# Small-head attention: per-head products of 32 rows in place of masked key copies, slots written out

## The reference

```python
scores = jnp.einsum('bqhd,bkhd->bhqk', Q, K) / scale     # 16 heads, d = 8
attn = jax.nn.softmax(scores, axis=-1)
out = jnp.einsum('bhqk,bkhd->bqhd', attn, V).reshape(B, T_q, D)
```

## Time and profile before

| | us |
|---|---|
| median of 3 runs | 1088.5 |
| lowest, highest | 1086.8, 1091.34 |
| span of the profiled execution | 1088.4 |
| TensorE matmuls busy | 889.5 |
| VectorE busy | 787.4 |
| ScalarE busy | 470.4 |
| GpSimd busy | 172.3 |

### The profile page before, as it was taken

One profiled execution on the slowest core, in us unless ns is written; L12 is line 12 of the kernel. 1 busy time (PEld: TensorE's weight loads), 2 busy tenths in 40 slices (PEclk: granted clock), 3 DMA queues, 4 the chain that ended last, 5 costly groups with the idle time before them and its releaser, 6 DMA issues. The chain is left out here.

```text
span 1088.4 us, 15120 instructions
## 1 busy us (share of the span) xinstructions
PE 889.5 (82%) x5078; PEld 654.4 (60%) x5078; DVE 787.4 (72%) x1420; ACT 470.4 (43%) x693; POOL 172.3 (16%) x139
## 2 busy tenths in 40 slices
PE   2688747767998998899966888469989975999997
PEld 2555535436676676777744555346766754777774
DVE  4688654766868767678876887768677665778875
ACT  1254422113454443289941545134544422555553
POOL 1000010003313222122230000133132211011112
PEclk9699966997999999699975999679999985999998
DMA  7000000030000000000110050000000000000000
GB/s 321 1 1 1 1 0 1 0 155 1 1 0 0 0 1 2 0 1 0 36 43 0 1 244 4 0 1 1 1 0 0 1 1 0 1 0 0 0 1 20
DMA packets 1916, 22.78 MB, mean 21 GB/s; under 512 B 208, under 2 KB 208, under 8 KB 1104
## 3 DMA queue, kind: packets, MB, share of 16 engines
q1 hardware_dynamic: 1872, 22.22, 5.0%
HBM read 21.69 MB, written 0.52 MB: 20 GB/s over the span
## 5 line engine op out<-in xcount | busy, mean ns | idle before, releaser
L180 PE MATMUL banks<-work_split 128*128 128x256 f32 (+1 forms) x420 | 153.7, 366 | 13.1 <-DVE work_split L1186 6.8
L180 PE MATMUL banks<-normed_t_high,work_split 128*128 128x512 f32 x260 | 113.7, 437 | 46.2 <-DVE normed_tokens L924 9.9
L181 PE MATMUL banks<-work_split 128*128 128x256 f32 (+1 forms) x420 | 140.3, 334 | 0.0
L182 PE MATMUL banks<-work_split 128*128 128x256 f32 (+1 forms) x420 | 140.2, 334 | 0.0
L855 POOL TENSOR_TENSOR work<-work 128x512 f32<-128x512 f32 x64 | 86.4, 1350 | 260.3 <-PE banks L700 167.0
L180 PEld LDWEIGHTS banks<-work_split 128*128 128x128 f32 x420 | 82.0, 195 | 65.4 <-issue 30.0
L182 PE MATMUL banks<-normed_t_high,work_split 128*128 128x512 f32 x260 | 107.7, 414 | 0.0
L181 PE MATMUL banks<-normed_t_low,work_split 128*128 128x512 f32 x260 | 107.3, 413 | 0.0
L524 DVE TENSOR_REDUCE work<-banks 128x2 f32<-128x512 f32 x128 | 84.9, 687 | 27.3 <-PE banks L359 26.9
L180 PEld LDWEIGHTS banks<-normed_t_high,work_split 128*128 128x128 f32 x260 | 51.4, 198 | 67.3 <-issue 27.4
L182 PEld LDWEIGHTS banks<-work_split 128*128 128x128 f32 x420 | 82.1, 196 | 7.9
(11 more groups left out here) (228 smaller groups left out, 1816.9 us busy)
## 6 DMA issues: line engine op xcount, KB each, us to landing
raw_b<-in_wf SPq DMA_DIRECT2D x1, 6528.0 KB, 19.6
raw_a<-in_wf SPq DMA_DIRECT2D x1, 4096.0 KB, 12.0
raw_a<-in_wf SPq DMA_DIRECT2D x1, 2048.0 KB, 13.0
raw_b<-in_wb SPq DMA_DIRECT2D x1, 2048.0 KB, 17.5
raw_a<-in_wb SPq DMA_DIRECT2D x1, 2048.0 KB, 7.9
small_operands<-in_small SPq DMA_DIRECT2D x1, 1600.0 KB, 7.1
residual<-in_x SPq DMA_DIRECT2D x1, 512.0 KB, 3.7
sublayer_out_t<-in_ctx_t SPq DMA_DIRECT2D x1, 512.0 KB, 7.9
```

The costliest lines, as they stand in the source:

```text
L180: nc.tensor.matmul(o, w[0], m[0], start=start, stop=False)
L181: nc.tensor.matmul(o, w[0], m[1], start=False, stop=False)
L182: return nc.tensor.matmul(o, w[1], m[0], start=False, stop=stop)
```

## The change

- The four masked copies are gone. The keys stay in one stacked buffer `a_ky`, now with four halves (the keys of steps x to x + 3), and the ones of rows 24 and 25 are added by ACT as a bias in `high`.
- A product for head j reads the 32 partitions of head j alone, of weights and of moving data, both in `maxima` and in `scores`.
- `maxima(x, n)` is one head (n % 4) with two query tiles of one sequence instead of one tile with two heads.
- `scores(x, u)` is one pair of heads with both key blocks of one sequence; head j always writes bank j. Scores 2 and 3 wait for the exponentials of 0 and 1. There are four probability buffers instead of two (two lie in `raw_a`, columns 6144 to 8191), and `values(x, b)` has eight products for a sequence instead of four: two groups per slot instead of four.
- The first four projections use banks 4, 5, 2 and 3, and do not wait for stacks.
- All eight slots of a call are written out, on PE, ACT and DVE.

```diff
-        A = signals("a", NG, w=2, q=4, hi=4, y=4, km=8, v=2, mx=16, red=16, m2=2, mt=2, yf=2, s=8, p=8, pv=8,
+        A = signals("a", NG, w=2, q=4, hi=4, y=4, v=2, mx=16, red=16, m2=2, mt=2, yf=2, s=8, p=8, pv=4,
...
-        a_y, a_yf, a_ky = wr[:, 0:1024], wr[:, 1024:2048], wr[:, 2048:3072]
-        a_km = [wr[:, 3072 + 1024 * j:4096 + 1024 * j] for j in range(GH)]
+        a_y, a_yf, a_ky = wr[:, 0:1024], wr[:, 1024:2048], wr[:, 2048:4096]
...
+        a_p += [raw_a[:, 6144 + 1024 * k:7168 + 1024 * k] for k in range(2)]
...
-        def small_passes(eng, slot):
-
-
-            with eng.Fori(0, NG - 2) as i:
-                slot(i, 0, True, True, True)
-                slot(i, 1, True, True, True)
-            slot(NG - 2, 0, True, True, True)
-            slot(NG - 2, 1, False, True, True)
-            slot(NG - 1, 0, False, False, True)
-            slot(NG - 1, 1, False, False, False)
+
+
+        STEPS = 2 * NG
+
+        def a_rows(j):
+            return slice(BLK * j, BLK * (j + 1))
+
+        def a_bank(x, k):
+
+            return (4, 5, 2, 3)[2 * x + k] if x < 2 else 5
...
+                if k and x >= 2:
+                    at("y", 2 * x + 1)
...
+                mm3(bank(a_bank(x, k)), (a_wh[:, k * P:(k + 1) * P], a_wl[:, k * P:(k + 1) * P]), src)\
+                    .then_inc(A["q"].sem, 1)
...
+            def maxima(x, n):
+                pair, j = n // GH, n % GH
                 if n == 0:
-                    at(i, "km", 4 * x + 4)
+                    at("y", 2 * x + 2)
                 if n >= 2:
-                    at(i, "red", 8 * x + n - 1)
-                for j in range(j0, j0 + 2):
-                    last = nc.tensor.matmul(ps[:, 6 + n % 2, (j % 2) * S:(j % 2 + 1) * S],
-                                            a_y[:, t * P:(t + 1) * P], a_km[j][:, (t // 2) * S:(t // 2 + 1) * S],
+                    at("red", 8 * x + n - 1)
+                for e in range(2):
+                    t = 4 * (x % 2) + 2 * pair + e
+                    last = nc.tensor.matmul(ps[:, 6 + n % 2, e * S:(e + 1) * S], a_y[a_rows(j), t * P:(t + 1) * P],
+                                            half(a_ky, x % 4)[a_rows(j), pair * S:(pair + 1) * S],
                                             start=True, stop=True)
                 last.then_inc(A["mx"].sem, 1)
...
             def scores(x, u):
+                b = u // 2
+                if u >= 2:
+                    at("p", 4 * x + u - 1)
+                for kb in range(2):
+                    for j in range(2 * (u % 2), 2 * (u % 2) + 2):
+                        last = nc.tensor.matmul(ps[:, j, kb * S:(kb + 1) * S],
+                                                half(a_ky, x % 4)[a_rows(j), b * S + kb * P:b * S + (kb + 1) * P],
+                                                half(a_yf, x % 2)[a_rows(j), b * S:(b + 1) * S],
+                                                start=True, stop=True)
...
+            def values(x, b):
+                if b == 0:
+                    at("v", x + 1)
+                at("p", 4 * x + 2 * b + 2)
+                for kb in range(2):
+                    for j in range(GH):
+                        last = nc.tensor.matmul(ps[a_rows(j), 4, b * S:(b + 1) * S],
+                                                a_vg[:, 4 * (x % 2) + 2 * b + kb, j, :],
+                                                a_p[2 * b + j // 2][:, (2 * (j % 2) + kb) * S:(2 * (j % 2) + kb + 1) * S],
+                                                start=kb == 0, stop=kb == 1)
...
+            def slot(x):
                 def more(*tiles):
+                    for n in tiles if x + 1 < STEPS else ():
+                        maxima(x + 1, n)
+
+                at("yf", x + 1)
                 scores(x, 0)
                 more(0, 1)
                 scores(x, 1)
                 more(2)
+                scores(x, 2)
                 more(3)
+                if x + 2 < STEPS:
+                    project(x + 2, 1)
                 more(4)
+                values(x, 0)
                 scores(x, 3)
+                more(5, 6, 7)
+                values(x, 1)
+                if x + 2 < STEPS:
+                    at("y", 2 * (x + 2) + 2)
+                sums_back(x)
+                if x + 1 < STEPS:
+                    maxima_back(x + 1)
+                if x + 3 < STEPS:
+                    at("att", x + 1)
+                    project(x + 3, 0)
...
+                at("q", 2 * x + k + 1)
+                if x >= 1:
+                    at("y", 2 * (x - 1) + k + 1)
+                src = bank(a_bank(x, k))
+                if k:
+                    ins = nc.scalar.activation(half(a_hi, k), src, ACT.Identity, bias=col("one_rows"))
+                else:
+                    ins = nc.scalar.activation(half(a_hi, k), src, ACT.Copy)
+                ins.then_inc(A["hi"].sem, 1)
...
+                    if u == 3 and x + 2 < STEPS:
+                        high(x + 2, 1)
+                    at("s", 4 * x + u + 1)
+                    if x:
+                        at("pv", 2 * (x - 1) + u // 2 + 1)
+                    nc.scalar.activation(a_p[u], bank(2 * (u % 2), 2), ACT.Exp,
                                          scale=float(1.0 / np.sqrt(np.float32(DH8)))).then_inc(A["p"].sem, 1)
+                at("pv", 2 * x + 2)
...
+                dst = half(a_ky, x % 4) if k else half(a_y, x % 2)
...
-            def masked_keys(i, x, heads=range(GH)):
-                at(i, "y", 2 * x + 2)
-                for j in heads:
-                    nc.vector.tensor_scalar(half(a_km[j], x % 2), half(a_ky, x % 2).bitcast(F32), col("one_rows"),
-                                            col("head", j, 1), ALU.add, ALU.mult).then_inc(A["km"].sem, 1)
...
+                t, j = 4 * (x % 2) + 2 * (n // GH), n % GH
...
+                if x % 2 == 1 and x // 2 + 2 < NG:
+                    small_weights(dve, c, x // 2 + 2, raw, r0)
...
+                if x + 1 < STEPS:
+                    minus(x + 1)
+                normalise(x)
+                if x + 1 < STEPS:
+                    queries(x + 1)
...
+    ones = ((r % BLK == 24) | (r % BLK == 25)).astype(f)[:, None]
+    put("lo_k", ones - ((r % BLK) // DH8 == 1).astype(f)[:, None])
+    put("one_rows", ones)
```

More of the change, by code:

```diff
@@ L405, in slot @@
                 more(2)
+                scores(x, 2)
                 more(3)
[L407 to L410, removed]
+                if x + 2 < STEPS:
+                    project(x + 2, 1)
                 more(4)
-                values(i, x, 1)
-                more(5)
+                values(x, 0)
                 scores(x, 3)
[L415 to L426, removed]
+                more(5, 6, 7)
[8 more added lines that the diff above has]
+                    project(x + 3, 0)
             for x in range(2):
                 pe.wait_ge(s_xs, 2 * splits(m) + x + 1)
[L430 to L433, removed]
+                project(x, 0)
+                project(x, 1)
             for n in range(8):
[L435 to L439, removed]
+                maxima(0, n)
+            maxima_back(0)
+            project(2, 0)
+            for x in range(STEPS):
+                slot(x)
         def small_act(act, c):
@@ L447, in small_act, with at @@
             vsrc = vsrc.rearrange("p (t d) -> p t d", t=NT)
[L449 to L458, removed]
+            def at(name, k):
+                act.wait_ge(A[name].sem, A[name].at(c, 0, k))
@@ L480, in small_act @@
+                if x + 3 < STEPS:
+                    high(x + 3, 0)
             act.wait_ge(s_ainit, c + 1)
             for x in range(2):
-                value_tiles(0, x)
+                value_tiles(x)
             for x in range(2):
                 for k in range(2):
-                    high(0, x, k, used=x == 1)
-            high(0, 2, 0)
-            small_passes(act, slot)
+                    high(x, k)
+            high(2, 0)
+            for x in range(STEPS):
+                slot(x)
@@ L515, in masked_keys, with at @@
[L515 to L524 removed]
+            def at(name, k):
+                dve.wait_ge(A[name].sem, A[name].at(c, 0, k))
@@ L581, in small_dve @@
+                stack(x, 1)
             small_weights(dve, c, 1, raw, r0)
             for n in range(8):
-                largest(0, 0, n)
+                largest(0, n)
             dve.wait_ge(s_ainit, c + 1)
-            minus(0, 0)
-            queries(0, 0)
-            with dve.Fori(0, NG - 2) as i:
-                order.loop(i, 4)
-                slot(i, 0, True, True, True)
-                slot(i, 1, True, True, True)
-            order.end(NG - 2)
-            slot(NG - 2, 0, True, True, True)
@@ L593, in small_dve @@
-            slot(NG - 2, 1, False, True, True)
-            slot(NG - 1, 0, False, False, True)
-            if before_last is not None:
-                before_last()
-            slot(NG - 1, 1, False, False, False)
+            minus(0)
+            queries(0)
+            for x in range(STEPS):
```

(3 more changed lines are left out.)

131 lines of the change are left out of this document (41 added, 90 removed).

## The result

The changed kernel takes **1144.6 us** (median of 4 runs, 1137.9 to 1152.6) against 1088.7 for the kernel before on the same chip (4 runs). The ratio is 1.051, 95% interval 1.048 to 1.054. The prediction said 1074.5, with a range from 1060 to 1085 and 0.08 for slower, so it is wrong in sign. The profiled execution took 1146.7 us, with a span of 1144.9.

What follows compares the result with a forecast made beforehand. It took chains between engines, not a full engine, as the bound, with PE's in-order queue late next. Prologue -16.0, slots +4.2, last slots +0.6, loop -1.4 and weight split -1.2 made -13.8: 1074.5 us, range 1060 to 1085.

Steps and rivals of the forecast that it cites:

- rival D: PE's extra waiting drops its clock: slots some 17 us, slower from a quarter of them, 1121 us with half; chance 0.07.
- Prologue: Start of each call: projections in separate banks, no key copies, first reduce sooner by 8.5 and 7.5 us.
- Masked copies in the slots: Removing DVE's key copies: pair before the reciprocal worth nothing, pair after the query sum under 0.2 us.
- rival B: DVE is the true bound and its 2.0 us leave all 12 slots with copies: 1048 us; chance 0.05.
- Value group of 16 records: In a slot, each of the two larger groups of value products takes 1.07 us, bounds 0.85 and 1.28.
- Pitch of scores: Spacing of 32-row score products in the slots: between 0.06 us with two heads alternating and 0.12 without overlap.
- Rival A: Row groups overlap fully, in the maxima too, with short borders: slots about 11.2 us, kernel 1065 us; chance 0.20.
- Borders: Where 32-row groups meet other PE groups in a slot: 0.2 us each; without the drain rule, 0.3 per slot less.
- Slot at the upper clock: From one `att` to the next, 11.64 us becomes 11.6 to 12.05, with PE's in-order queue late next.
- Loop: Writing out the slots saves 0.17 us in four slots per call, -1.4 us for both calls.
- Weight split hidden: The weight split, 0.45 us in two slots per call, falls mostly into DVE's new idle time: -1.2 us.
- Last slot: The last slot of each call has a longer value group at its end: +0.3 us each, +0.6 in all.

Runs made afterwards that it cites:

- masks_gpsimd: Kernel before with new banks for the first four projections, slots written out and the slots' masked key copies made on GpSimd: 1081.7 us, ratio 0.992.
- masked_new: Changed kernel with masked key copies on DVE put back and full-row products of them, in the new order: 1092.8 us, ratio 1.001.
- filled_tail: Changed kernel plus unread full-row products in PE's waits, fewer at a slot's end, more in the last two slots: 1083.0 us, ratio 0.993.
- all_rows: Changed kernel with maxima and scores products reading all 128 rows, no masks, head separation left out: 1083.97 us, ratio 0.995.
- banks_unrolled: Kernel before with banks 4, 5, 2, 3 for the first four projections and the loop's slots written out: 1085.3 us, ratio 0.995.
- narrow_twice: Changed kernel with every 32-row product of maxima and scores issued twice into the same place: 1183.7 us.

## Why the prediction was wrong, and where it was right

**The step that failed** is the clock under the slots. The sum took every slot of rows 5 at the upper level and left the lower one to rival D, with a chance of 0.07. I read the slot after 113.14 as PE having waited and then fallen, and asked only how much more PE would wait. What decided was which rows its products read: the same order with full rows, PE busy 79% of a slot and down to 59% in the last, keeps the upper clock, and 32-row products lose it at 81%. No row of the trace before shows a 32-row product; I bounded its pitch from both sides and never its effect on the clock. D's price of a slot was right: "a slot some 17 us" against 16.90. Its point of decision holds too: 14 slots between the first and last `att` of both calls took 16.9 eight times and 12.1 to 16.0 otherwise; more than a quarter were slow and the kernel is slower. Its total for half of the slots, 1121 us, is too low, since the other six were at the lower level as well for all or part of their length. D's mechanism, waiting, is not what the runs show for the changed kernel. For the one slot of rows 8 and 9, where full-row products fell to the lower level, no run tests it. That D named the right size of a slot by another mechanism is luck.

The Trainium skill (TensorE: Matmul & The Clock Gate, Part 1) lets the chip set the clock by how busy PE has been. By PE's busy share in the profile the rows differ from this: with the clock up, 32-row products lost it at 81% and full ones kept it at 79% and 59%. The measurement decides: the busy share alone does not tell the level.

Point by point:

- *Prologue*, -8.5 and -7.5 predicted: -8.5 and -7.9 measured.
- *Masked copies in the slots*, nothing and under 0.2: 0.34 by masks_gpsimd, 0.2 by masked_new. A bit more than I gave, and far from rival B's 2.0; DVE is not the bound.
- *Value group of 16 records*, 1.07 predicted: 1.07 in filled_tail and all_rows; 1.94 at the lower clock.
- *Pitch of scores*, 0.06 to 0.12: eight score products of the four heads take 0.53 us at the upper clock (row at 62.11), while four full ones take 0.64. Less an end of 0.28 that is 0.04 a product, under both bounds. One product by itself takes as long as a full one (0.28 us); the gain is in the overlap. Rival A's overlap is real, as the Trainium skill has it (TensorE: Matmul & The Clock Gate, Part 3), but slots did not fall to 11.2 by it.
- *Borders*, 0.2 each and 0.3 per slot: not measured by themselves. all_rows has none between 32-row and full groups, and its slots (11.98) are no shorter than those of filled_tail (11.84 on average), so nothing shows them on the path, though these two kernels differ in more than the borders.
- *Slot at the upper clock*, 11.6 to 12.05: 11.62 and 12.06 with filling, 11.98 in all_rows. Had the clock held, the sum was sound.
- *Loop*, 0.17 a slot: 0.14 to 0.16. No run shows the 1 us allowed at worst for fetching code: in banks_unrolled the first slot of a call takes 11.96 us, the third 11.97.
- *Weight split hidden*, -1.2: half right. In filled_tail slots with it are 0.44 longer than those without, as before; in all_rows and in the changed kernel it is hidden.
- *Last slot*, +0.3: 9.51 in all_rows against 8.97, +0.5.
- *Sum*: from the median of 1088.5 the terms, -13.8, give 1074.7 and not 1074.5; this changes nothing.

The slots account for the loss. From the first reduce to the last `att` call 1 took 98.96 us before and 130.10 after, call 2 98.13 and 134.69: +31.1 and +36.6, less 16.4 of the prologues leaves +51.3, of +56.5 in the span. The other 5 us lie outside these stretches, 2.2 of them in stretch 2, which the change does not touch.

The gains of the good versions come out smaller than their stages say, for that reason: all_rows is 12.5 us shorter in the two stretches with the calls, but its profiled span is 7.1 below that of the kernel before. Other stretches are longer (198.0 against 194.9 and 126.8 against 124.6, stretches 3 and 4), with the same code. In both the granted clock is lower: 0.940 against 0.955, and 0.877 against 0.884. In stretch 3 that is about 6.4 us more at the lower level, which at half speed costs at most 3.2 us, an estimate that meets the 3.1 measured; in stretch 4 it would account for about half. That the shift in time brings this about is my reading, and no run separates it.

**Open.** Why the clock rises in slots 4 and 5 of call 1 (0.61, 0.73) and in every other slot of narrow_twice (0.59), and stays at 0.50 in call 2 of the changed kernel. Products of 64 rows were not tried, nor narrow weights by themselves; value products with 32 weight columns stand in every kernel here, those at 1.00 too.

## What to carry to other kernels

Before cutting products down to fewer rows, ask what will hold the clock up: here full-height products over zeros kept PE at the upper level, and narrow ones, though quicker in groups, let it fall for all work around them, from 11.5 to 16.9 us a slot. Read the granted clock by window first, and when it is low at a high busy share, look at the shapes as well as at the waits. An engine's removed work is worth only what the chain to the next meeting point shows: 2.0 us of DVE gave 0.34.

## What the hardware did that I had not expected

- The clock by rows, above: 0.50 in most slots with all score and maxima products on 32 rows (PE busy 83 to 88%), 0.87 with half of them, 1.00 with none (79%), and 1.00 in all slots but one with ten full products a slot added.
- GpSimd's copy of 128x512 takes 786 ns. While it runs beside DVE's two small operations on 128x16, those take 580 and 331 ns instead of 186 and 183. Moving two of the four copies behind them brought both back.
- Narrow products of different heads do overlap: eight in 0.53 us. And they do not start in the order of the queue. The eight at 62.11 are scores 0 and 1 of a step, between which maxima 0 and 1 stand in PE's program; these start at 62.45, behind both. Scores 1 read the rows of the third and fourth head, maxima 0 and 1 those of the first and second, on which scores 0 were still running. In all_rows, where all read 128 rows, the order is that of the program:

```profile
60.30 0.64 PE L379 MATMUL banks<-work_split 128*128 128x256 f32 x4
60.77 0.64 PE L361 MATMUL banks<-work_split 128*128 128x256 f32 x4
61.25 0.28 PE L379 MATMUL banks<-work_split 128*128 128x256 f32 x1
```
